# Token experts: every fourth block of Gelu's result split by GpSimd from a copy in SBUF

## What is computed

```python
def _ffn(h, w1, b1, w2, b2):
    return jax.nn.gelu(h @ w1 + b1, approximate=False) @ w2 + b2
def _token_moe(h, gw, gb, w1, b1, w2, b2):
    cw = _combine_weights(h @ gw + gb)        # softmax over the top 2 of 8 experts
    out = jnp.zeros_like(h)
    for e in range(E):
        out = out + _ffn(h, w1[e], b1[e], w2[e], b2[e]) * cw[..., e:e + 1]
    return out
```

## Time and profile before

| | |
|---|---|
| median of 3 runs | 3146.79 us (3143.51 to 3146.86) |
| the profiled execution, its own time | 3150.18 us |
| its span | 3148.5 us |
| PE busy | 2659.7 us, 84% |
| DVE busy | 2638.5 us, 84% |
| ACT busy | 2248.2 us, 71% |
| POOL busy | 588.9 us, 19% |

### The profile page before, as it was taken

One profiled execution on the slowest core, in us unless ns is written; L12 is line 12 of the kernel. 1 busy time (PEld: TensorE's weight loads), 2 busy tenths in 40 slices (PEclk: granted clock), 3 DMA queues, 4 the chain that ended last, 5 costly groups with the idle time before them and its releaser, 6 DMA issues. The chain is left out here.

```text
span 3148.5 us, 71461 instructions
## 1 busy us (share of the span) xinstructions
PE 2659.7 (84%) x28144; PEld 1162.4 (37%) x28144; DVE 2638.5 (84%) x3552; ACT 2248.2 (71%) x4330; POOL 588.9 (19%) x1125
## 2 busy tenths in 40 slices
PE   3469999899799995759999999579998998899976
PEld 3332333577423333412222222222333776323325
DVE  5758899788798995769999999389998887899976
ACT  1137888676578884439999999458988676689864
POOL 3123100344321001100000000032101543321011
PEclk8668999999899997969999999789999998899998
DMA  1061000215310000230000000150000314300001
GB/s 33 1 149 41 23 14 14 59 45 108 73 31 21 14 12 25 67 70 9 13 12 14 12 12 12 49 114 25 16 16 15 74 51 98 73 22 18 15 12 31
DMA packets 109883, 119.09 MB, mean 38 GB/s; under 512 B 20726, under 2 KB 87660, under 8 KB 109548
## 3 DMA queue, kind: packets, MB, share of 16 engines
q1 hardware_dynamic: 102444, 98.21, 12.3%
q0 software_dynamic: 4608, 13.96, 2.4%
q10 hardware_dynamic: 2496, 2.36, 0.4%
HBM read 70.31 MB, written 43.78 MB: 36 GB/s over the span
## 5 line engine op out<-in xcount | busy, mean ns | idle before, releaser
L1480 ACT ACTIVATE h_probsf<-h_ps_lowf 128x512 f32<-128x512 f32 (+3 forms) x812 | 424.3, 551 | 131.3 <-PE h_ps_lowf L1414 80.2
L1480 ACT ACTIVATE h_probsg<-h_ps_lowg 128x512 f32<-128x512 f32 (+3 forms) x812 | 424.3, 551 | 118.2 <-PE h_ps_lowg L1414 76.5
L1480 ACT ACTIVATE h_probsb<-h_ps_lowb 128x512 f32<-128x512 f32 x683 | 389.1, 596 | 79.4 <-PE h_ps_lowb L1414 61.2
L1435 PE MATMUL h_ps_valuesf<-h_probsf,v_all 128*9 128x256 f32 (+2 forms) x4608 | 354.2, 380 | 40.3 <-POOL h_probsf L1578 33.1
L1435 PE MATMUL h_ps_valuesg<-h_probsg,v_all 128*9 128x256 f32 (+2 forms) x4608 | 350.2, 376 | 30.2 <-POOL h_probsg L1578 22.8
L1435 PE MATMUL h_ps_valuesb<-h_probsb,v_all 128*9 128x256 f32 x4096 | 318.4, 383 | 9.3 <-ACT h_drainedb L1489 5.0
L1528 DVE TENSOR_REDUCE h_maxima_0b<-h_ps_scanb 128x2 f32<-128x1024 f32 x256 | 292.4, 1213 | 29.9 <-PE h_ps_scanb L1376 29.9
L1528 DVE TENSOR_REDUCE h_maxima_2b<-h_ps_scanb 128x2 f32<-128x1024 f32 x256 | 292.7, 1214 | 6.7 <-PE h_ps_scanb L1376 6.7
L1528 DVE TENSOR_REDUCE h_maxima_0f<-h_ps_scanf 128x2 f32<-128x1024 f32 x224 | 259.1, 1216 | 21.8 <-PE h_ps_scanf L1376 21.2
L1528 DVE TENSOR_REDUCE h_maxima_0g<-h_ps_scang 128x2 f32<-128x1024 f32 x224 | 258.7, 1215 | 19.3 <-PE h_ps_scang L1376 18.6
L1480 ACT ACTIVATE h_probsf<-h_ps_highf 128x512 f32<-128x512 f32 (+3 forms) x404 | 224.1, 555 | 38.0 <-PE h_ps_lowf L1414 35.2
(11 more groups left out here) (483 smaller groups left out, 5230.5 us busy)
## 6 DMA issues: line engine op xcount, KB each, us to landing
q_stack<-combine_weights SPq DMA_DIRECT2D x64, 256.0 KB, 3.6
q_stack<-in_L_ffn_e_w SPq DMA_DIRECT2D x24, 256.0 KB, 3.2
q_stack<-q_parts SPq DMA_DIRECT2D x22, 256.0 KB, 6.0
k_stack<-k_parts SPq DMA_DIRECT2D x22, 256.0 KB, 8.2
attended<-h_drainedf SPq DMA_DIRECT2D x16, 256.0 KB, 2.9
attended<-h_drainedf SPq DMA_DIRECT2D x32, 128.0 KB, 1.9
attended<-h_drainedb SPq DMA_DIRECT2D x32, 128.0 KB, 1.9
attended<-h_drainedg SPq DMA_DIRECT2D x16, 256.0 KB, 2.2
```

The lines of the kernel that those rows point to most:

```text
L1435: last = nc.tensor.matmul(ps_values[32 * j:32 * j + VD, low:high], m.v_all[:, kb, QUAD * quad + j, :], probs[:, (u + j % banks) % RING_P, ...
L1480: nc.scalar.activation(by_head(probs[:, of % RING_P, :], of), by_head(ps_scores[of % RING_S], of), ACT.Exp, scale=SOFTMAX_SCALE).then_inc( ...
```

## The change

`by_pool(k)` is true for the token experts, from block 32 on, where k % 4 is 1 (`POOLED`): 24 blocks of each feed forward. For such a block

- ScalarE computes Gelu once, into a new buffer `gelu_sb` in SBUF. It no longer waits for the down product, but for the split of the block 4 before, as there is one such buffer;
- VectorE's `low(k)` is left out;
- GpSimd runs `split_hidden(k)`: it waits for Gelu and for the down product of block k - 4, casts to `hidden_hi`, and subtracts into `hidden_lo`. It stands behind all work for expert y = k // 4 - 2;
- TensorE's `up(k + 4)` waits for Gelu alone, and `down(k)` for GpSimd.

The counts in the other waits are adapted (`lows`, `pooled`, `doubled`).

```diff
+        def by_pool(k):
+            return by_token and k >= blocks and k % FB == POOLED
...
+            def split_hidden(k):
+                pool.wait_ge(gelu_ready, k + 1)
+                pool.wait_ge(down_ready, k + 1 - RING_SPLIT)
+                nc.gpsimd.tensor_copy(hidden_hi[:, k % RING_SPLIT, :], gelu_sb[:, :]).then_inc(high_by_pool, 1)
+                pool.wait_ge(high_by_pool, pooled(k))
+                nc.gpsimd.tensor_tensor(hidden_lo[:, k % RING_SPLIT, :], gelu_sb[:, :],
+                                        hidden_hi[:, k % RING_SPLIT, :].bitcast(F32), ALU.subtract).then_inc(split_by_pool, 1)
...
                     if e == EXPONENTIAL and c + 1 < CHUNKS:
                         exponential(c + 1)
+                    k = FB * (y + 2) + POOLED
+                    if k < total and by_pool(k):
+                        split_hidden(k)
...
             def low(k):
+                if by_pool(k):
+                    return
...
                 if k >= RING_H:
-                    pe.wait_ge(low_ready, k + 1 - RING_H)
+                    if by_pool(k - RING_H):
+                        pe.wait_ge(gelu_ready, k - RING_H + 1)
+                    else:
+                        pe.wait_ge(low_ready, lows(k - RING_H))
...
-                pe.wait_ge(low_ready, k + 1)
+                if by_pool(k):
+                    pe.wait_ge(split_by_pool, pooled(k))
+                else:
+                    pe.wait_ge(low_ready, lows(k))
...
+                if by_pool(k):
+                    if pooled(k) > 1:
+                        act.wait_ge(split_by_pool, pooled(k) - 1)
+                    nc.scalar.activation(gelu_sb[:, :], ps_h[:, k % RING_H, :], ACT.Gelu, bias=bias).then_inc(gelu_ready, 1)
+                    return
...
-                    act.wait_ge(high_by_act, k // 2 + 1)
+                    act.wait_ge(high_by_act, doubled(k))
```

More of the change, by code:

```diff
@@ L1882 @@
 CLEAR_AT = 4
+POOLED = 1
 FIRST_COMBINED, FIRST_WEIGHTS, FIRST_ROWS, LATE_SPLITS = 5, 8, 3, 3
```

8 lines of the change are left out of this document (added).

## The result

| | before | after |
|---|---|---|
| median of 6 runs | 3146.82 us (3143.24 to 3149.61) | 3156.75 us (3152.09 to 3160.32) |
| ratio, 95% interval | | 1.0027 [1.0015, 1.0039] |
| the profiled execution, its own time | 3150.18 us | 3152.09 us |
| its span | 3148.5 us | 3150.4 us |

The change makes the kernel 0.27% slower, where 0.14% had been forecast: 8.5 us by the ratio and 9.9 by the medians, against 4.4. The median forecast was 3151.2 us, in a range of 3141.0 to 3158.0. By the prediction's own mark of 0.2% a change of 0.27% counts as slower, to which it gave 0.32, and not "same", its likeliest outcome.

The account below looks back on a forecast made before the run. TensorE was taken to set the time, hardly ever idle in chunks 1 to 3. Per feed forward -1.15 + 0 + 0.6 + 2.75 = +2.2 us, twice +4.4, from 3146.79 to 3151.2 us, range 3141.0 to 3158.0.

Parts of the forecast that it names:

- A: TensorE's 1.15 us wait at block 46: block 41's single Gelu lets VectorE come sooner; gain 1.15 us.
- B: TensorE's 1.59 us wait at block 56: choosing the second expert still ends with GpSimd's addition; no gain, 0.
- Elsewhere: Remaining blocks: splits end before their down products want them or are covered, VectorE's other subtractions aren't slowed; no loss.
- C: TensorE's 2.37 us wait at block 88: normalising the next layer's chunk 1 ends later beside GpSimd; loss 0.6, bound 1.3.
- D: TensorE's 2.87 us wait at the next layer's chunk 2 turn: power 1.3 later, normalising 1.45 longer; loss 2.75 us.
- idle at B as before: Sign to look for in the changed kernel's profile: TensorE's wait at block 56 unchanged, 1.59 us before.
- The clock I leave as it is: TensorE's stretches at 1.2 GHz were taken as unchanged, since the long waits stay long.
- The rival "clock": Longer idle around D brings one more half-clock stretch per feed forward, +3.4 us in all, 3154.6 us; chance 0.26.
- stand back to back and catch three: At C, GpSimd's subtraction, multiplication and addition hold up three of VectorE's four normalising operations.
- Near 3 us: Sign to look for: how long the four normalising operations at C take after the change, 2.59 us before.
- The cover at block 81: Split up to 1 us late, hidden by the wait at C; all such cover gone costs 1.7 us per feed forward.
- the relief rival: GpSimd's operations fit VectorE's gaps, -4.1 us, and a half-clock stretch at C goes, 1.7 more: 3141.0 us; chance 0.18.

Follow-up runs that it names:

- no_109_113: The changed kernel, but blocks 109 and 113 split as before the change (Gelu twice, VectorE subtracts); ratio to the kernel before 1.0002.
- only_41: The kernel before, with only block 41 of each feed forward split by GpSimd; ratio to the kernel before 0.9978.
- no_113: The changed kernel, but block 113 alone split as before the change; ratio to the kernel before 1.0016.
- no_85_89: The changed kernel, but blocks 85 and 89 split as before the change; ratio to the kernel before 1.0023.
- power_first: The changed kernel, with GpSimd's power ahead of the same expert's multiplication and addition (y = 10, 18, 26); ratio to the kernel before 1.0023.
- before_two_more: The kernel before, with a GpSimd cast and subtraction into an unread spare buffer behind the power of expert 26; ratio to the kernel before 1.0004.
- quiet_110: The changed kernel, with the power first for y = 26 and GpSimd then waiting until VectorE has normalised; ratio to the kernel before 0.9996.
- only_41_power_early: As only_41, with the power for chunk 2 moved ahead of the loads of the next layer's stacks; ratio to the kernel before 0.9978.
- before_quiet: The kernel before, no block split by GpSimd, with the three rearrangements of only_41_quiet; ratio to the kernel before 0.9964.
- only_41_quiet: As only_41 with quiet_110's edit, plus exponential ahead of experts 11 and 19, and GpSimd waiting for normalising before expert 20; ratio to the kernel before 0.9949.

## Why the forecast was right in direction and short in size

The balance by the prediction's own terms, per feed forward, in us (measured: first, last feed forward):

| term | forecast | measured |
|---|---|---|
| A, to block 46 | -1.15 | -1.31, -1.32 |
| B, 46 to 64 | 0 | +0.05, -0.23 |
| 64 to 84 (in "Elsewhere") | 0 | +0.41, +0.44 |
| C, 84 to 92 | +0.6 | +3.20, +1.12 |
| 92 to 112 | 0 | -0.05, -0.02 |
| D, 112 to 127 | +2.75 | +3.79, +3.16 |
| sum | +2.2 | +6.09, +3.15 |

**A was right**, mechanism and size. Without the wait for a product and without the second Gelu, nothing is idle at block 46. The kernels with block 41 alone show both halves. The gain, 1.31 us at block 46 and 1.41 at 47, is above the 1.15 us of recorded idle time. An estimate from the rows: the records of two matmuls overlap by 0.39 - 0.23 = 0.16 us, and the one behind a matmul that waited starts 0.33 instead of 0.23 us behind it, so a wait costs some 0.26 us more than is shown for it.

**B was right** as a sum, and in part by luck: 0.5 and 0.7 us are gained up to block 56, and 0.5 of them lost again by block 64 in each feed forward. The sign that was named for it, idle at B as before, failed: it is 0.52 us at block 56 and not 1.59. The choice did end sooner, and what took it back is a step that the prediction doesn't have: GpSimd's operations caught the small ones that combine the weights (L1753 1.18 us instead of 0.89, L1755 1.14 instead of 0.19, L1756 0.52 instead of 0.19).

**D was right in its mechanism and in each of its two pieces.** Counted from up product 112, the power started 4.93 us later before and 6.22 after, 1.29 us more (forecast 1.3). Normalising took 2.47 us instead of 1.11, 1.36 more (forecast 1.45; with its bound of 1.5 the bounds add to 2.8, not to the 2.85 written). The turn moved from 7.25 to 9.91 us behind that product, 2.66 (forecast 2.75). The wait for block 109's split, 1.45 us, took the place of a part of the turn's, as written. The step that fell short is "The clock I leave as it is": behind D the half clock lasted 6.8 us instead of 3.4 in both feed forwards. That is the rest, 1.1 and 0.5 us, of this term. The rival "clock" had this mechanism, at 1.7 us per feed forward, and let it hang on the idle time around D doubling; that rose from 2.87 to 5.3 us, not quite twice.

**C was mis-sized**, at +0.6, in three steps. First, the operations "stand back to back and catch three". They caught four: the cast of block 89 came right behind the addition, and I had not followed GpSimd's queue that far. Normalising took 4.24 us. "Near 3 us" was forecast, and even that doesn't fit the forecast's own ends, 0.6 us sooner and 0.6 later, which make it 3.8. Second, it did not start 0.6 us sooner. Counted from up product 83 it started 9.89 us later instead of 9.91, and ended 1.63 later than before: the choice of chunk 3 was not "as in B" but ended 0.57 us later, since one more of its operations was caught (L1736, 1.33 us instead of 0.19), and that ate the subtraction left out. Third, in the first feed forward a stretch at half clock came behind block 90 (1.6 of its 3.2 us are lost from block 90 to 92). The bound of +1.3 covers the last feed forward (1.12), which has no such stretch, but not the first.

**The cover at block 81 held in part.** Its split comes late, and TensorE waits 0.97 us for it at 729.96. Up product 86 starts 1.25 us later for it, and at block 88, where TensorE waits for VectorE anyway, 0.7 us of that are back in the first feed forward and 1.1 in the last. This stands within the term C. At block 49 TensorE waits 0.45 us in the first feed forward, ahead of B.

**The loss from block 64 to 84 is another catch**, at a place where the forecast had looked only at the splits' down products and at VectorE's subtractions. Behind block 77 VectorE works out the mean and variance of the next layer's chunk 1, on 128x4 values. GpSimd now does block 77's split at that moment. VectorE and GpSimd of after:

```profile
718.00 0.52 DVE L309 TENSOR_TENSOR mean<-st 128x4 f32<-128x4 f32 x1
...
718.75 1.14 DVE L311 TENSOR_SCALAR next_tmp<-next_tmp 128x4 f32<-128x4 f32 x1
...
717.89 0.61 POOL L2025 CAST e_hidden_hif<-e_geluf 128x512 fp32r<-128x512 f32 x1
718.58 1.28 POOL L2027 TENSOR_TENSOR e_hidden_lof<-e_geluf,e_hidden_hif 128x512 fp32r<-128x512 f32 x1
```

In the kernel before each of these takes 0.17 us. VectorE is 1.3 us later for them, and up product 83 starts 0.4 us later, released by VectorE's low part. No kernel leaves out block 77 alone, so this rests on the rows.

Against the forecast of +4.4 us the balance has 4.8 more over both feed forwards: C 3.1, D 1.4 and the stretch from 64 to 84 0.9, less 0.6 from the others. The time lands where the rival "clock" with C at its upper bound was put, 3156 us. That is in part luck. The rival's own step came true, 3.4 us more at half clock at each D, but not its size, 1.1 and 0.5 us where it had 1.7, and C was far above its bound in one feed forward.

How much of the loss is clock can't be said exactly, since at half clock TensorE also waits less. 6.8 us more at half clock are worth 3.4 us of work. What a stretch of 3.4 us costs depends on where it lies. Behind a single wait of 2.8 to 2.9 us at D, blocks 112 to 127 take 28.4 to 28.8 us with one and 27.2 without, so 1.2 to 1.6 us. At C of before, the stretch began at about 2586.6, ahead of the end of TensorE's wait at 2587.07, not behind it as the prediction reads it: blocks 84 to 112 take 46.78 us there and 46.65 in the first feed forward, which has none. So the 1.7 us that the relief rival counted on for losing it were not there to be had.

What stays open: why no_109_113, with the same wait of 2.87 us at the turn as the kernel before, has no stretch at half clock there, and only_41 has one at C of the last feed forward but none at D. Seen over the one profiled execution of each kernel, the four kernels with a wait both at the down product of block 109 and at the turn (after, no_113, no_85_89, power_first) have a stretch at D in each of their two feed forwards, 8 of 8. The six with the wait at the turn alone (before, before_two_more, no_109_113, and three with block 41 alone) have one in 7 of 12, and the length of that wait doesn't sort them: before_two_more has 4.21 us there and no more half clock than before. quiet_110, with the wait at 109 alone, has none. What decides a single one isn't shown. Whether the four loads' issue alone holds VectorE up, as only_41_power_early suggests (its first normalising operation took 1.31 us beside it), wasn't tried by itself.

## What to carry to other kernels

Work moved to GpSimd is not judged by busy time. Look at what VectorE runs beside it. Here operations with two inputs in SBUF, and TENSOR_SCALAR from SBUF to SBUF, were held until GpSimd's operation of 128x512 ended, while those that read PSUM, and TENSOR_REDUCE, weren't. Where such short VectorE operations lie on the path, put GpSimd's work ahead of them or let it wait for them. Here one such wait in each feed forward made nearly all of the difference between power_first and quiet_110, 8.4 and -0.7 us. Follow the queue of the moved work past the operation at hand, to the one behind it, and VectorE's queue to every short operation, not only to those ahead of a known wait: that is what catches and is caught.

## What the runs showed of the hardware

- Four TENSOR_SCALAR of 128x128 in SBUF on VectorE take 1.11 us alone. Beside a stream of GpSimd's, as many of them as GpSimd has operations last until one of those ends: 2.47 us beside a cast and a subtraction (two held), 4.24 beside three of two inputs and a cast (four held), 4.55 beside three of two inputs and a cast in another order.
- A cast of one input on GpSimd (0.61 us) holds VectorE as well as a subtraction does (the last of the four at block 85 in the kernel after is recorded with 0.63 us, and alone with 0.34).
- Not everything in SBUF is held. TENSOR_REDUCE of 128x32 took 0.18 to 0.19 us in all 11 cases in chunks 1 to 3 of the kernel after where it began inside an operation of GpSimd on 128x512, as here:

```profile
677.34 0.18 DVE L1734 TENSOR_REDUCE q_stack<-q_stack 128x4 f32<-128x32 f32 x1
...
677.21 1.29 POOL L2040 TENSOR_TENSOR q_stack<-q_stack 128x512 f32<-128x512 f32 x1
```

- Nor does everything on GpSimd hold. Beside the power on 128x4 (1.02 us, from 678.07 in the kernel before) L1735 and L1736, of two inputs in SBUF, took their 0.19 us.
- The level of 1.2 GHz came in stretches of 3.4 or 6.8 us within the experts. With two waits of 1.45 and 3.87 us at D it lasted 6.8; with waits of 1.45 and 2.50 it lasted 3.4 (no_113). The waits alone don't set it: no_85_89 has 3.4 us in the first feed forward and 6.8 in the last, with the same waits to 0.05 us. In before_quiet and only_41_quiet, whose waits at D are gone, there was none in chunks 1 to 3. All of this is from one execution of each kernel.
